# Layer norm, low-rank attention and a mixture of experts on one core: the order of GpSimd's work and of the score pairs, copies two steps later, low-rank rows in one DRAM block, the first steps written out

## The chip, the cores and the metric

One core of a Trainium2 chip runs the whole program. The metric is the device time of one execution in microseconds, the median of several runs. Engines: PE (TensorE), DVE (VectorE), ACT (ScalarE), POOL (GpSimd) and SP (SyncE), which issues most DMAs.

## The reference, cut to what matters

The input x is 8 batches of 512 tokens of width 256. All is float32.

```python
xn = layernorm(x)
def holo_linear(x, basis, phase, amp):           # basis 32x256, phase and amp 256x32
    return (x @ basis.T) @ (amp * cos(phase)).T  # rank 32
q, k, v = (heads(holo_linear(xn, ...)) for each)           # 16 heads of 16
attn = holo_linear(softmax(q @ k.T / 4) @ v, *o)
y = sum over the best 2 of 8 experts: share * (silu(xn @ w_gate) * (xn @ w_up)) @ w_down   # F = 352
shared = (silu(xn @ sw_gate) * (xn @ sw_up)) @ sw_down     # F = 704, every token
out = x + attn + y + shared
```

## The kernel before, in words

The kernel has three stages. **Preparation**: normalised rows go to DRAM (xn_rows) and, transposed and split, to xn_T_split; the tokens are routed and sorted by expert; the last batch's low-rank rows (low_rank_first) and its q and k rows are made. The low-rank rows are the 3 x 32 = 96 products of xn with the bases of q, k and v. Numbers are kept as a high and a low part, and a product takes the pairs high-high, low-high, high-low. **Tiles**: 71 tiles of 128 sorted tokens run through their expert, and expert_rows holds the results. **Attention**: 8 batches (b; the data come last batch first) of 4 head groups (g) of 8 steps (t), called a slot (b, g). `slots` calls one function per engine for (-1, 3), a slot without attention of its own that makes what (0, 0) needs, and then for all others.

In each step PE makes two pairs of score matmuls. The *score pair* (`score`, L1363, into s_pair) holds q times k for a later slot, four steps to a slot ahead; DVE takes its maximum over keys (`maximum`, L1867), and only then may the next score pair start, as there is one s_pair. The *transposed pair* (`score_T`, L1437, into st_pair) holds k times q of the present slot with the maxima as additional rows; ACT takes its exponential (`exponent`, L1082), and only then may the next one start. In before, `next_score` goes first in steps with t % 4 other than 0, and `score_T` first in steps 0 and 4. The matmuls of values with the exponentials (`values`, L1449) are in steps 0 and 4. Between them PE does pieces of the shared SwiGLU of the same or next batch: `gate_up_shared` (L1409) for hidden tiles 0 to 4 of 128 columns, 24 matmuls in 4 pieces over 4 steps, `gate_up_both` for the last tile of 64 ("odd"), then `down_pair` (L1512). Step 2 or 6 also has one small matmul group: a projection of the next batch's q or k (`project`, L1353), the output projection, the low-rank rows of batch b + 2 (`low_rank`, L1463) or the values.

Of a SwiGLU tile q: ACT takes the tanh and a halved copy of `up`, DVE multiplies (`gate_shared`, L1882), POOL multiplies by `up` (`hidden`, L777), ACT copies the high part (`hidden_high`, L1063, in steps 1 and 5), POOL makes the low part (`hidden_low`, L785). Tile 4 of a batch is in slot (b, 1), second half, and so is the odd tile.

POOL's work is one list written by hand: per batch the four `hidden` and `hidden_low`, the gathers of expert rows (`gather_y`, L802, each a DMA that POOL issues), their sums (`sum_y`, L809 to L814), and for each half of the heads `normalise` (L793, after a broadcast of the inverse sums, o_sum, comes back from DRAM) and `ao_low` (L797). Each waits in order.

SP's work is a list too. In slot (b, 3) it stores the high low-rank rows of b + 2 (L607), waits for DVE's low part, stores that (L609), loads the maxima into q_rows (`load_max`, L632, after ACT's copy of the turned maxima at L1041), loads q and k rows three slots ahead (`load_rows`, L557), and reloads the low-rank rows in the layout of the projections (`load_low_rank`, L616), for which it first waits until both stores have landed (semaphore r_st). In `slot_first` it loads rows of group 1, stores low rank 1, loads the maxima, reloads low rank 1 and loads rows of group 2. In the preparation (L504, L507) it does the same two stores, and ACT waits for them before it writes over their source (L940).

Memory: w_sh, xT_b1 and what follows them in the stage `late` lie over the first experts' weights, which are free when the last experts run.

Of the kernel before, what the change touches and what calls it, by code (L numbers as in the profile page):

```python
# [6 lines left out]
P = 128  # L7
# [8 lines left out]
HI, LO = 0, 1  # L16
# [47 lines left out]
def build_program(nc, x, attn, gate_w, w_gate, w_up, w_down, sw_gate, sw_up, sw_down, out):  # L64
# [36 lines left out]
    r_dram = nc.dram_tensor("low_rank_rows", (2, 32, 3, L), F32).ap()  # L101
# [11 lines left out]
    with ctx:  # L113
# [108 lines left out]
        xT_1 = sb("xT_b1", [P, 2, KT, L], F32R, late)  # L222
        r_hi = sb("r_hi", [96, L], F32R, late)
# [6 lines left out]
        q_rows = [None] + [sb(f"q_rows{g}", [P, 2, L], F32R, late) for g in range(1, NG)]  # L230
        k_rows = [None] + [sb(f"k_rows{g}", [P, 2, L], F32R, late) for g in range(1, NG)]
# [176 lines left out]
        def slots(slot):  # L408

            slot(-1, 3)  # L410
            for b in range(NB):
                for g in range(NG):
                    slot(b, g)
# [48 lines left out]
        def _(sp):  # L462
# [44 lines left out]
            sp.dma_start(r_dram[LO].rearrange("h n l -> n h l"), e_lo[0][0:96, :].bitcast(F32)).then_inc(r_st, 16)  # L507
# [52 lines left out]
            def load_first_values():  # L560
                for c, part in enumerate((HI, HI, LO)):
                    sp.dma_start(r_rows[0][c * HARM:(c + 1) * HARM, 2, :].bitcast(F32), r_dram[part, :, 2, :]).then_inc(r_in, 16)
# [41 lines left out]
            def store_low_rank(b):  # L604
                wait(sp, r_in, b * 48)
                wait(sp, a_r, b + 1)
                sp.dma_start(r_dram[HI].rearrange("h n l -> n h l"), r_hi[:, :].bitcast(F32)).then_inc(r_st, 16)  # L607
                wait(sp, d_r, b + 1)
                sp.dma_start(r_dram[LO].rearrange("h n l -> n h l"), r_lo[:, :].bitcast(F32)).then_inc(r_st, 16)  # L609

            def load_low_rank(b):
# [3 lines left out]
                for c, part in enumerate((HI, HI, LO)):  # L615
                    sp.dma_start(r_rows[b % 2][c * HARM:(c + 1) * HARM, :, :].bitcast(F32), r_dram[part]).then_inc(r_in, 16)  # L616
# [99 lines left out]
        def _(pool):  # L716
# [103 lines left out]
            def last_group(b):  # L820
# [7 lines left out]
                if there(b + 1):  # L828
                    hidden_low(b + 1, 0)
                    gather_at(b + 1, 1, 3, 6) if there(b) else gather_y(0, 1)  # L830

            last_group(-1)
            for b in range(NB):
                hidden(b, 1)
                gather_at(b, 2, 0, 1)
                hidden_low(b, 1)
                sum_y(b, 0)
                gather_at(b, 3, 0, 3)
                hidden(b, 2)
                gather_at(b, 4, 0, 5)  # L840
                hidden_low(b, 2)
                sum_y(b, 1)
# [3 lines left out]
                hidden_low(b, 3)  # L846
# [1170 lines left out]
```

## Time and profile before

| | us |
|---|---|
| runs, median (lowest to highest) | 995.96 (995.03 to 998.99) |
| the profiled execution's own time | 991.98 |
| its span, first to last instruction | 990.2 |
| mean granted clock of TensorE, share of 2.4 GHz | 0.950 |
| preparation, up to the first tile | 94 |
| tiles | 278 |
| attention, from its first shared matmul at 374.4 | 616 |

A span is from the first instruction to the last of one profiled execution; the time of that execution has some 2 us around it. An engine's busy time says how much it had to do, and the waits say what it stood for. A busy matmul row is not a matmul at its peak, since ends of pipelined matmuls are modelled.

### The profile page before, as it was taken

Reading aid. Unit: us, or ns where it says so; the run is one execution under the profiler, and the core shown is the slowest. Engines: PE = TensorE matmul, PEld = TensorE weight load, DVE = VectorE, ACT = ScalarE, POOL = GpSimd, SP = SyncE. Lnnn points to the kernel's source line nnn. Section 1 sums busy time; section 2 is a strip of 40 time slices with the busy share of each in tenths; the row PEclk is TensorE's granted clock in tenths of the full one; section 3 lists DMA queues with packets and bytes.
Section 4 is the critical chain, followed back from the end, with each engine's and each line's share of the span. In section 5 each row is a group of like instructions: output and inputs, shape, how many; then the busy total and the mean of one; then the engine's idle time right before and its main releaser. Section 6 shows DMA issues by size and latency. Waiting matters only on the chain.

```text
span 990.2 us, 19557 instructions
## 1 busy us (share of the span) xinstructions
PE 882.8 (89%) x6491; PEld 616.1 (62%) x6492; DVE 613.8 (62%) x923; ACT 580.6 (59%) x935; POOL 407.1 (41%) x411
## 2 busy tenths in 40 slices
PE   4745999999999986999999998989989999989996
PEld 3435999999999974555464464555455555446452
DVE  7867834434443454776776775766766686776762
ACT  4746644444444433757757756756756766766764
POOL 2003522222222233825825815733833752752831
PEclk9965999999999998999999999989999999999999
DMA  9983655222222126464565655554655664644411
GB/s 314 382 253 136 209 144 168 74 73 70 69 74 70 47 91 148 143 166 129 171 173 134 185 153 131 163 154 121 182 153 128 175 167 117 184 125 99 107 31 43
DMA packets 89928, 140.04 MB, mean 141 GB/s; under 512 B 17304, under 2 KB 51616, under 8 KB 87936
## 3 DMA queue, kind: packets, MB, share of 16 engines
q1 hardware_dynamic: 83168, 121.24, 42.4%
q0 software_dynamic: 6480, 17.70, 6.7%
q8 instruction: 44, 0.72, 0.3%
q14 instruction: 28, 0.23, 0.1%
q10 hardware_dynamic: 208, 0.14, 0.0%
HBM read 79.24 MB, written 54.71 MB: 135 GB/s over the span
## 4 chain that ended last, share of the span: by engine, by line
PE 59%; DMA 18%; DVE 7%; POOL 5%; ACT 4%; issue 4%; SPq 3%; DVEq 0%; ACTq 0%; POOLq 0%
PE s_pair L1290 8%; PE bank L1308 8%; PE bank L1512 7%; PE bank L1449 6%; PE st_pair L1290 6%; PE s_pair L1363 4%; PE bank L1409 4%; DMA low_rank_rows<-ro 4%; PE st_pair L1437 4%; DMA r_rows<-low_rank_rows 3%; DMA o_sum<-inverse_rows 3%; DMA inverse_rows<-o_inv 2%; PE bank L1298 2%; DVE top L1867 2%; PE bank L1273 2%
## 5 line engine op out<-in xcount | busy, mean ns | idle before, releaser
L1867 DVE TENSOR_REDUCE top<-s_pair 128x2 f32<-128x1024 f32 x248 | 303.8, 1225 | 166.6 <-PE s_pair L1363 159.0
L1082 ACT ACTIVATE prob<-st_pair 128x1024 f32<-128x1024 f32 x252 | 258.3, 1025 | 109.4 <-PE st_pair L1437 105.6
L755 POOL DMA_INDIRECT xg<-xn_rows,token_of x71 | 78.5, 1106 | 216.7 <-PE bank L1273 161.9
L1409 PE MATMUL bank<-xT_b,w_sh 64*128 64x512 f32 x960 | 146.5, 411 | 0.4
L1363 PE MATMUL s_pair<-k_rows,q_rows 48*128 48x512 f32 x496 | 117.8, 469 | 13.1 <-DVE top L1867 10.8
L1437 PE MATMUL st_pair<-q_rows,k_rows 50*128 50x512 f32 x504 | 109.2, 428 | 19.7 <-ACT prob L1082 11.0
L1449 PE MATMUL bank<-prob,v_ones 128*32 128x512 f32 x1024 | 126.5, 613 | 0.0
L1409 PEld LDWEIGHTS bank<-xT_b,w_sh 64*128 64x128 f32 x960 | 93.6, 191 | 30.7 <-issue 8.4
L793 POOL TENSOR_TENSOR ao<-ao,o_sum 128x512 f32<-128x512 f32 x15 | 19.3, 1287 | 183.6 <-DMA o_sum<-inverse_rows 183.6
L1308 PE MATMUL bank<-w_exp,c_hT 128*128 (+1 forms) x639 | 94.2, 292 | 0.3 <-ACT c_y L994 0.3
L777 POOL TENSOR_TENSOR h_f<-h_f,u_half 128x512 f32<-128x512 f32 x40 | 51.6, 1291 | 92.3 <-DVE h_f L1882 92.0
L1290 PE MATMUL s_pair<-w_exp,xg_T 128*128 x468 | 88.6, 339 | 0.0
L1363 PEld LDWEIGHTS s_pair<-k_rows,q_rows 48*128 48x128 f32 x496 | 48.8, 191 | 63.8 <-DVE top L1867 48.2
L1308 PEld LDWEIGHTS bank<-w_exp,c_hT 128*128 128x128 f32 (+1 forms) x639 | 81.2, 190 | 0.7 <-issue 0.6
L1512 PE MATMUL bank<-w_sh,h_T 64*128 64x256 f32 x1088 | 80.4, 282 | 1.3 <-DVE ro L1934 1.1
L1512 PEld LDWEIGHTS bank<-w_sh,h_T 64*128 64x128 f32 x1088 | 75.0, 185 | 9.9 <-issue 3.0
L1290 PEld LDWEIGHTS s_pair<-w_exp,xg_T 128*128 128x128 f32 x468 | 77.7, 195 | 0.3
L1437 PEld LDWEIGHTS st_pair<-q_rows,k_rows 50*128 50x128 f32 x504 | 49.5, 191 | 42.2 <-ACT prob L1082 20.2
L1290 PE MATMUL st_pair<-w_exp,xg_T 128*128 x384 | 70.7, 333 | 0.0
L989 ACT ACTIVATE c_hT<-bank 128x384 fp32r<-128x384 f32 x71 | 34.9, 491 | 59.3 <-PE bank L1298 59.3
L802 POOL DMA_INDIRECT y_b<-expert_rows,slot_of x64 | 64.1, 1002 | 12.0 <-issue 7.5
L1449 PEld LDWEIGHTS bank<-prob,v_ones 128*32 128x32 f32 x1024 | 27.2, 111 | 62.5 <-issue 57.1
(230 smaller groups left out, 1249.9 us busy)
## 6 DMA issues: line engine op xcount, KB each, us to landing
qk_rows<-qk_hi SPq DMA_DIRECT2D x56, 256.0 KB
q_rows<-qk_rows SPq DMA_DIRECT2D x64, 192.0 KB
k_rows<-qk_rows SPq DMA_DIRECT2D x56, 192.0 KB
expert_rows<-c_y SPq DMA_DIRECT2D x71, 128.0 KB, 1.7
xn_T_split<-x_T SPq DMA_DIRECT2D x8, 1024.0 KB, 6.6
xT_b<-xn_T_split SPq DMA_DIRECT2D x7, 1024.0 KB, 8.6
qk_rows<-qk_lo SPq DMA_DIRECT2D x28, 256.0 KB
x_all<-in_L_attn_x_dram SPq DMA_DIRECT2D x8, 512.0 KB, 8.1
```

The source lines that it names most:

```text
L755: pool.indirect_dma_start(xg[s % 4][:, :], None, xn_dram, bass.IndirectOffsetOnAxis(token_of[:, s:s + 1], 0)).then_inc(c_x[s % 4], 16)
L777: pool.tensor_tensor(h, h, u_half[:, :], ALU.mult).then_inc(p_hf, 1)
L802: pool.indirect_dma_start(y_b[:, t % 2, k, :], None, y_dram, bass.IndirectOffsetOnAxis(slot_of[:, k, of(b) * TPB + t:of(b) * TPB + t + 1], ...
L1082: act.activation(prob[n % 3][:, 2 * jp:2 * jp + 2, :].rearrange("p j l -> p (j l)"), score_T_pair(b, g, t)[:, :], ACT.Exp, scale=HD ** -0. ...
L1290: ins = pe.matmul(gu_bank_of(s, i)[n][:, 0:F], xg_T[i % 2][:, a * KT + k, :], w, start=(m == 0 and k == 0), stop=(m == 2 and k == KT - 1))
L1308: ins = pe.matmul(y_bank[:, 0:D], c_hT[i % 2][0:n, a, k, :], w, start=(m == 0 and k == 0), stop=(m == 2 and k == FT - 1))
L1363: ins = pe.matmul(score_pair(b, g, v)[:, i * 512:(i + 1) * 512], q_rows[g][r:r + 48, jp, qt * P:(qt + 1) * P], k_rows[g][r:r + 48, jp, :], ...
L1409: ins = pe.matmul((g_bank, u_bank)[up][:, :], w_sh[rows, a, o:o + P], xT_of(b)[rows, c, k, :], start=(n == 0 and i == 0), stop=(n == 1 and ...
L1437: ins = pe.matmul(score_T_pair(b, g, t)[:, i * 512:(i + 1) * 512], k_rows[g][r:r + QK_ROWS, jp, kt * P:(kt + 1) * P], q_rows[g][r:r + QK_R ...
L1449: ins = pe.matmul(ot_bank[32 * j:32 * j + 32, :], v_ones[:, kt, 4 * g + j, :], prob[(b * 16 + g * 4 + kt) % 3][:, j, :], start=(kt == 0), ...
L1512: ins = pe.matmul((g_bank, u_bank)[to][:, 0:D], h_T[rows, a, f, t * P:(t + 1) * P], w_sh[rows, c, S_GU + f * D:S_GU + (f + 1) * D], start= ...
L1867: dve.tensor_reduce(top[g % 2][:, :, jp, qt], score_pair(b, g, v)[:, :].rearrange("p (i k) -> p i k", i=2), AX_X, ALU.max).then_inc(d_max, 1)
```

## The change

- r_dram, low_rank_rows, is (2, 96, 512) in place of (2, 32, 3, 512): the stores write it as it lies, and the reload picks rows n * 32 + h.
- q_rows1 and k_rows1 get a place directly behind xT_b1, and load_rows(0, 1) is issued after the store of tile 66, behind load_xT(1).
- POOL: in each batch sum_y(0), sum_y(1) come before hidden_low 1, 2; normalise(b-1, 1) and gather 7 before hidden_low 3; sum_y(2) behind hidden 4 and ao_low; gather 1 of the next batch before its hidden_low 0.
- ACT: hidden_high in steps 3 and 7 in place of 1 and 5.
- PE: score_T first in every step.
- slot(-1, 3) goes; its work is written out for PE, DVE and ACT, and low_rank(1) comes behind turn_max(0, 0) and score(0, 1, 0).

```diff
-    r_dram = nc.dram_tensor("low_rank_rows", (2, 32, 3, L), F32).ap()
+    r_dram = nc.dram_tensor("low_rank_rows", (2, 96, L), F32).ap()
...
         xT_1 = sb("xT_b1", [P, 2, KT, L], F32R, late)
+        q_rows1 = sb("q_rows1", [P, 2, L], F32R, late)
+        k_rows1 = sb("k_rows1", [P, 2, L], F32R, late)
...
         def slots(slot):
 
-            slot(-1, 3)
             for b in range(NB):
...
-            sp.dma_start(r_dram[HI].rearrange("h n l -> n h l"), e_hi[0][0:96, :].bitcast(F32)).then_inc(r_st, 16)
+            sp.dma_start(r_dram[HI], e_hi[0][0:96, :].bitcast(F32)).then_inc(r_st, 16)
...
                 if s == 66:
                     load_xT(1)
+                    load_rows(0, 1)
...
-                sp.dma_start(r_dram[LO].rearrange("h n l -> n h l"), r_lo[:, :].bitcast(F32)).then_inc(r_st, 16)
+                sp.dma_start(r_dram[LO], r_lo[:, :].bitcast(F32)).then_inc(r_st, 16)
...
-                    sp.dma_start(r_rows[b % 2][c * HARM:(c + 1) * HARM, :, :].bitcast(F32), r_dram[part]).then_inc(r_in, 16)
+                    sp.dma_start(r_rows[b % 2][c * HARM:(c + 1) * HARM, :, :].bitcast(F32), r_dram[part].rearrange("(n h) l -> h n l", n=3)).then_inc(r_in, 16)
...
             def slot_first():
-                load_rows(0, 1)
+                load_max(0, 0)
                 store_low_rank(1)
-                load_max(0, 0)
+                load_rows(0, 2)
                 load_low_rank(1)
-                load_rows(0, 2)
...
                 if there(b + 1):
+                    gather_at(b + 1, 1, 3, 6) if there(b) else gather_y(0, 1)
                     hidden_low(b + 1, 0)
-                    gather_at(b + 1, 1, 3, 6) if there(b) else gather_y(0, 1)
...
                 gather_at(b, 2, 0, 1)
+                sum_y(b, 0)
                 hidden_low(b, 1)
-                sum_y(b, 0)
...
                 gather_at(b, 4, 0, 5)
+                sum_y(b, 1)
                 hidden_low(b, 2)
-                sum_y(b, 1)
...
                 gather_at(b, 6, 1, 1)
-                hidden_low(b, 3)
                 if there(b - 1):
                     normalise(b - 1, 1)
-                sum_y(b, 2)
                 gather_at(b, 7, 1, 3)
+                hidden_low(b, 3)
                 hidden(b, 4)
                 if there(b - 1):
                     ao_low(b - 1, 1)
+                sum_y(b, 2)
                 hidden_low(b, 4)
...
-                    if t % 4 == 1 and what == "pair":
+                    if t % 4 == 3 and what == "pair":
                         hidden_high(c, q)
...
+            max_rows(0, 0)
             low_rank_high(1)
-            max_rows(0, 0)
+            tanh(0, 0)
+            up_half(0, 0)
+            values_out(0, 0)
+            hidden_high(0, 0)
             slots(slot)
...
                     score(0, 0, run)
-                    low_rank(1)
                     down(NS - 1, END - 1, at[run + 1])
-                    turn_max(0, 0)
...
                     wait(pe, a_mt, b * NG + 1)
+                    if b == 0:
+                        pe.wait_ge(d_r, 2)
...
                 for t in range(STEPS):
-                    if t % 4:
-                        next_score(b, g, t)
                     if now:
                         score_T(b, g, t)
+                    next_score(b, g, t)
                     if t % 4 == 0:
-                        next_score(b, g, t)
                         piece(b, g, t, 4)
...
             some_tiles(NS // RUN * RUN, last=True)
+            turn_max(0, 0)
+            score(0, 1, 0)
+            low_rank(1)
             pe.wait_ge(c_yk, NS)
             pe.wait_ge(c_hed, NS)
+            for n in range(3):
+                gate_up_shared(0, 0, n)
+            score(0, 1, 1)
+            gate_up_shared(0, 0, 3)
+            score(0, 1, 2)
+            project_values(0, 0)
+            score(0, 1, 3)
+            for n in range(4):
+                gate_up_shared(0, 1, n)
 
             slots(slot)
...
             split_max(0, 0)
+            maximum(0, 1, 0)
             low_rank_low(1)
+            maximum(0, 1, 1)
             dve.wait_ge(c_yk, NS)
             dve.memset(v_ones[:, :, :, HD:2 * HD], 1.0).then_inc(ones_ok, 1)
+            maximum(0, 1, 2)
+            gate_shared(0, 0)
+            maximum(0, 1, 3)
```

## Rows read from the trace of the kernel before

**Rows 1.** The page, part 1: busy us, share of the span, instructions by engine
```profile
PE 882.8 (89%) x6491; PEld 616.1 (62%) x6492; DVE 613.8 (62%) x923; ACT 580.6 (59%) x935; POOL 407.1 (41%) x411
```

**Rows 2.** Windows: stretch, its length, busy us and count by engine, PEclk, DMA share, GB/s
```profile
461.79:914.35 452.56, 419.99 (x3294) 238.52 (x3295) 316.74 (x371) 297.04 (x400) 233.35 (x228) 0.97 0.57 152
914.35:948.77 34.42, 32.03 (x218) 16.06 (x218) 24.13 (x27) 25.47 (x35) 30.32 (x31) 1.00 0.37 93
498.40:516.47 18.07, 17.70 (x202) 12.69 (x203) 14.13 (x19) 10.05 (x12) 2.11 (x3) 1.00 0.62 177
516.47:533.87 17.40, 17.39 (x131) 9.66 (x127) 12.29 (x15) 12.16 (x16) 6.51 (x6) 1.00 0.27 76
```

**Rows 3.** Waits of PE in 388 to 990: us in total, times, longest
```profile
PE st_pair L1437 <- ACT prob L1082: 11.0, 9, 2.2
...
PE bank L1353 <- DMA r_rows<-low_rank_rows: 9.3, 6, 2.3
PE st_pair L1437 <- DMA q_rows<-top_T: 8.3, 6, 2.0
```

**Rows 4.** Timeline of SP: start, us, DMA; the seam from batch 2 to 3
```profile
601.06 0.69 SPq L609 DMA_DIRECT2D low_rank_rows<-ro  x1
603.24 1.48 SPq L632 DMA_DIRECT2D q_rows<-top_T  x2
...
609.09 1.25 SPq L616 DMA_DIRECT2D r_rows<-low_rank_rows  x3
```

**Rows 5.** The page, part 6: DMA issues, KB each, us to landing
```profile
expert_rows<-c_y SPq DMA_DIRECT2D x71, 128.0 KB, 1.7
```

**Rows 6.** Window while the two low-rank stores run, columns as in rows 2
```profile
600.00:606.00 6.00, 6.00 (x47) 2.99 (x45) 4.71 (x8) 4.87 (x9) 2.98 (x3) 1.00 0.22 57
```

**Rows 7.** Timeline of PE at the same seam: start, us, group, idle before and its releaser
```profile
609.76 0.49 PE L1437 MATMUL st_pair<-q_rows,k_rows 50*128 50x512 f32 x2 [1.39 <-DMA q_rows<-top_T]
...
617.33 0.50 PE L1353 MATMUL bank<-r_rows,w_rows 96*128 96x512 f32 x1 [2.27 <-DMA r_rows<-low_rank_rows]
```

**Rows 8.** Timeline of all engines in the preparation
```profile
59.10 0.76 PE L1231 MATMUL bank<-e_qk,w_rows 96*128 96x512 f32 x1 [4.40 <-issue]
...
62.90 1.08 ACT L940 ACTIVATE e_hi<-bank 128x512 fp32r<-128x512 f32 x2 [4.82 <-DMA low_rank_rows<-e_lo]
```

**Rows 9.** Timeline of all engines in slot (3, 1)
```profile
638.77 1.29 POOL L793 TENSOR_TENSOR ao<-ao,o_sum 128x512 f32<-128x512 f32 x1 [2.47 <-DMA o_sum<-inverse_rows]
640.03 1.83 POOL L809 TENSOR_SCALAR y_b<-y_b,share 128x256 f32<-128x256 f32 x2
...
644.69 1.28 POOL L777 TENSOR_TENSOR h_f<-h_f,u_half 128x512 f32<-128x512 f32 x1
...
646.00 0.63 ACT L1063 ACTIVATE h_T<-h_f 128x512 fp32r<-128x512 f32 x1 [3.37 <-POOL h_f L777]
```

**Rows 10.** The page, part 5: DVE's maxima; busy us, mean ns | idle before
```profile
L1867 DVE TENSOR_REDUCE top<-s_pair 128x2 f32<-128x1024 f32 x248 | 303.8, 1225 | 166.6 <-PE s_pair L1363 159.0
```

**Rows 11.** Timeline of PE, steps 3 to 6 of slot (1, 3)
```profile
523.81 0.39 PE L1363 MATMUL s_pair<-k_rows,q_rows 48*128 48x512 f32 x2
...
525.57 0.50 PE L1437 MATMUL st_pair<-q_rows,k_rows 50*128 50x512 f32 x2
525.90 0.40 PE L1363 MATMUL s_pair<-k_rows,q_rows 48*128 48x512 f32 x2
...
528.30 0.50 PE L1363 MATMUL s_pair<-k_rows,q_rows 48*128 48x512 f32 x2
...
530.13 0.50 PE L1363 MATMUL s_pair<-k_rows,q_rows 48*128 48x512 f32 x2
```

**Rows 12.** Timeline of PE, from the last tile to slot (0, 0)
```profile
374.39 3.39 PE L1409 MATMUL bank<-xT_b,w_sh 64*128 64x512 f32 x24
380.02 0.80 PE L1363 MATMUL s_pair<-k_rows,q_rows 48*128 48x512 f32 x2 [2.24 <-DMA q_rows<-qk_rows]
...
388.71 0.40 PE L1437 MATMUL st_pair<-q_rows,k_rows 50*128 50x512 f32 x2
```

More of the change, by code:

```diff
@@ L229, in build_program @@
         qk_lo = [sb(f"qk_lo{i}", [P, L], F32R, late) for i in range(2)]
-        q_rows = [None] + [sb(f"q_rows{g}", [P, 2, L], F32R, late) for g in range(1, NG)]
-        k_rows = [None] + [sb(f"k_rows{g}", [P, 2, L], F32R, late) for g in range(1, NG)]
+        q_rows = [None, q_rows1] + [sb(f"q_rows{g}", [P, 2, L], F32R, late) for g in range(2, NG)]
+        k_rows = [None, k_rows1] + [sb(f"k_rows{g}", [P, 2, L], F32R, late) for g in range(2, NG)]
         u_half = sb("u_half", [P, L], F32, late)
@@ L561, in load_first_values @@
                 for c, part in enumerate((HI, HI, LO)):
-                    sp.dma_start(r_rows[0][c * HARM:(c + 1) * HARM, 2, :].bitcast(F32), r_dram[part, :, 2, :]).then_inc(r_in, 16)
+                    sp.dma_start(r_rows[0][c * HARM:(c + 1) * HARM, 2, :].bitcast(F32), r_dram[part, 2 * HARM:3 * HARM, :]).then_inc(r_in, 16)
             def store_y(s, i):
@@ L1114, in slot @@
                         up_half(c, q)
-                    if t == 5 and there(nb) and now:
+                    if t == 5 and there(nb):
                         max_rows(nb, ng)
@@ L1133, in slot @@
                         qk_high(b + 1, PROJECTED.index((g, t)))
-                    if g == 3 and t == 2 and there(b + 2) and now:
+                    if g == 3 and t == 2 and there(b + 2):
                         low_rank_high(b + 2)
@@ L1369, in turn_max @@
                 more = there(b + 1)
-                if g == 0:
+                if (b, g) == (0, 0):
+                    pe.wait_ge(c_hed, NS - 1)
+                elif g == 0:
                     wait(pe, d_r, b + 2) if more else wait(pe, d_po, (b - 1) * 2)
@@ L1456, in low_rank @@
                 wait(pe, xT_in, b * 16)
-                if b == 2:
-                    wait(pe, a_mt, 4)
+                if b <= 2:
+                    wait(pe, a_mt, 1 if b == 1 else 4)
                 else:
@@ L1568, in next_score @@
                 if t < STEPS - AHEAD:
-                    if there(nb) and there(b):
+                    if there(nb):
                         score(nb, ng, t + AHEAD)
@@ L1593, in small @@
                     project_o(b - 1, t // 4)
-                if g == 3 and t == 2 and there(b + 2) and there(b):
+                if g == 3 and t == 2 and there(b + 2):
                     low_rank(b + 2)
@@ L1614, in slot @@
                         values(b, g, 1)
-                    if t == 4 and there(nb) and now:
+                    if t == 4 and there(nb):
                         turn_max(nb, ng)
@@ L1939, in slot @@
                     if t < STEPS - AHEAD:
-                        if there(nb) and now:
+                        if there(nb):
                             maximum(nb, ng, t + AHEAD)
@@ L1943, in slot @@
                         maximum(qb, qg, t - STEPS + AHEAD)
-                    if t == STEPS - AHEAD - 1 and there(nb) and now:
+                    if t == STEPS - AHEAD - 1 and there(nb):
                         split_max(nb, ng)
@@ L1959, in slot @@
                         qk_low(b + 1, PROJECTED.index((g, t - 1)))
-                    if g == 3 and t == 3 and there(b + 2) and now:
+                    if g == 3 and t == 3 and there(b + 2):
                         low_rank_low(b + 2)
```

4 lines of the change are left out of this document (2 added, 2 removed).

## The prediction

> **What bounds the kernel now.** I read the page first, then the PE's waits in the attention phase, then windows of one batch, then the timelines round each wait. PE is busy 89% of the span; no other engine is over 62% [rows 1]. So time can only be had where PE stands still or has to go slower, and the windows say how much that is. Batches 1 to 6 take 452.56 us, 75.4 each. The same 32 steps without a stop are found in pieces: groups 0 and 1 in batch 7 (34.42), group 2 of batch 1 (18.07), group 3 of batch 1 up to its last wait (17.40), together 69.9 [rows 2]. Six times 75.4 minus 69.9 is **33 us** of stops and of half-speed PE behind them, for these six batches.
>
> The waits name three of the stops [rows 3]: the transposed score pair for ScalarE's exponential (11.0 us, 9 times), the first projection of the next batch for its low-rank rows (9.3, 6 times), the transposed pair for the maxima in q_rows (8.3, 6 times). Once or twice a batch each: these are seams, not the regular step. They sum to 28.6, and a granted clock of 0.97 in the mean, where 1.00 is 2.4 GHz [rows 2], holds most of the remainder of the 33.
>
> **Low-rank rows in one DRAM block.** At the end of a batch SP stores the high half, waits, stores the low half at 601.06, issues the maxima at 603.24 and can issue the reload only at 609.09, since it waits for the stores to land [rows 4]: 8 us for 192 KB. A 128 KB store of expert rows lands in 1.7 us [rows 5]. From 600 to 606 us the DMA share is 0.22, and the stream is little else than these two stores [rows 6]: 3 of 16 engines would be 0.19. The stored view is (3, 32, 512). The changed one is (96, 512). What it will use no row of before shows.
> The Trainium skill, "DMA: Bandwidth & Descriptors", section on why a DMA increments by 16, lets the slowest dimension of both access patterns set the number of engines, the largest divisor up to 16: 3 before, 16 after. The trace agrees with its first half (0.22 against 3/16).
> The bounds of one store are 1.7 us (the expert rows) and the present 8. I take 2.5: same size and shape class as the expert rows, half as large again. The reload then goes out straight behind the row loads, about 607 in place of 609.09, and the three stores' engines are free for the maxima. The reload itself turns from 6 KB into 2 KB pieces with 32 partitions outermost as before; I cost that between -0.5 and +1 us a batch, at 0.
> - Maxima: issued at 603.24, they held the pair until 609.76, after 1.39 idle [rows 7]. Two or three us of landing make them early by 2: all of 8.3 goes. SP's issue time doesn't move, since it waits for ScalarE's copy.
> - Projection: stopped 2.27 until 617.33 [rows 7]. Without the first stop PE is there at 613.7 (617.33 - 2.27 - 1.39); the reload, issued at 607 and landing 8 us later as now, would still be 1.3 late, and with less queued before it about in time. I let 2 of the 9.3 us stand.
> - Once more in the preparation: ScalarE stood 4.82 us for the low store, until 62.90, while the PE's first projection it copies ended at 59.10 + 0.76 [rows 8]. It starts at 59.9: **3.0 us**, and the inversion chain, the gathers and the tiles behind it all start from there. Bounds: 0, if another load is as late; 4.8, if the operands come earlier too.
>
> **GpSimd's order and the copies two steps later.** In group 1, GpSimd's normalise waits 2.47 for o_sum and ends at 640.06; then come the sum of expert rows from 640.03 on, a gather, and the product for SwiGLU tile 4 only at 644.69, so ScalarE, in order, stands 3.37 before its copy at 646.00 with the exponentials of two steps behind it [rows 9]. The new order puts before that product, after the same normalise, only gather 7 and hidden_low 3. The latter is 1.3, a tile like the products; the gather at most 1.5, what the 4.66 from 640.03 to 644.69 leave after 1.83 for two products and two additions of half a tile (0.65 each). So it begins by 642.9 and ends by 644.1. And the copy is asked for after the exponential of step 7, two steps or 4 us later (69.9 / 32 is 2.2 a step). So the stop of 3.37 has 1.8 + 4 to hide in. Late next are: ao_low for the output projection in step 7 (644.1 + 1.3 = 645.4, where it now ends at 647.3), hidden_low 4 behind the sum (3.2 and 1.3 more, 649.9; needed in step 2 of group 2, some 3 us later), and tanh of the odd tile, which needs hidden_low 3 (642.9, asked for in step 6). All pass, the first by the least. GpSimd's total is unchanged. The 11.0 us go, and I keep 1 us for a batch in which o_sum is later.
>
> **The transposed pair first.** Costed at nothing, by the steps themselves. DVE's maximum takes 1.23 us [rows 10], and score pair to score pair takes at least 1.82 (528.30 to 530.13) [rows 11]. Now the pair goes from step 3 to step 4 in 2.09 (523.81 to 525.90), since the transposed pair of step 4 goes ahead; afterwards by 1.82: 0.27 won. At step 4 to 5, 2.40 now, a transposed pair (0.33, 525.57 to 525.90) gets ahead: 0.33 lost [rows 11]. Net +0.06 for a half slot, up to 62 of them: +4. Where step 3 is bound otherwise, the 0.27 may be more or less. I take 0, bounds -5 and +20 (the 0.33 lost 62 times, nothing won).
>
> **First steps written out.** From the first shared gate matmuls to the first transposed pair PE takes 14.3 us (374.39 to 388.71) [rows 12]. Of that 6.8 are the two tiles' 48 matmuls (3.39 each) and about 1.6 four score pairs and the values; 5.9 are waits, 2.24 of them for q_rows that SP loads only after the last expert rows, and half-speed matmuls (a pair at 0.80 [rows 12], elsewhere 0.50 [rows 11]). The loads move ahead into tile 66; four DMAs of 0.4 us (three take 1.25 [rows 4]) between two stores cost nothing, since a tile takes 278 / 71 = 3.9. Low rank 1 moves from before the last down projection to behind the maxima's turn: neutral, and its cover is DVE's reading of the next scores. New waits: four maxima (4 x 1.23), a memset, the low-rank difference and one gate run in one DVE chain, with PE between them; I count 1 to 1.5 us of PE idle. Gain **5**, bounds 1 and 7.
> Of the queues: SP now issues the maxima of group 0 first, then the two low-rank stores, the rows of group 2, and the reload; the row loads (four, 0.4 each) cover the stores' landing, on which SP stood before. The values' projection gets a wait for DVE's low-rank difference, since both use one bank; it stands two score pairs behind it in the order, so it is costed at nothing, and 1 us if DVE is late.
>
> **The sum**, against the profiled execution's own 991.98 (span 990.2): preparation -3, first steps -5, seam waits 8.3 + 7.3 + 10 = -25.6, half-speed stretches that followed them -3 (of the 33 - 28.6 = 4.4), order 0. **-37, that is 955.** The runs' median, 995.96, is 4 above the profiled one; half of that may be its own. I say **958**.
>
> **Rivals.**
> - *Half the seams stay* (0.22). The reload still comes late, or o_sum does, which GpSimd waits for in every batch. For: both are behind the loads of q and k rows, and a faster PE asks sooner. Against: the copies have 4 us to spare. 25.6 / 2 or 13 us come back, and 1 for the clock: 972.
> - *The first steps run at half speed* (0.06). Their gaps are about 1.5 us in 12; the same work before, with 2.24 in one piece, had pairs of 0.80. Then 6.8 us of gate matmuls take some 4 more, and the gain is 1: 962. The Trainium skill, "TensorE: Matmul & The Clock Gate", Part 1, calls the slow clock the default, which activity releases; it would expect this wherever PE has been idle for long. The trace agrees here with its slow pairs behind the 2.24 us.
> - *The store stays on few engines* (0.05). 8.3 + 9.3 + 3 and some clock stay: 980. Against: the view's outer dimension is plainly 96.
> - *Every wait goes, with the half-speed stretches behind them* (0.15). All 33, and 6 to 7 before: 946.
> - *No net gain* (0.04). Maxima and waits eat it: 990 to 995.
> - *Slower: DVE's chain takes over* (0.04). With pairs evenly spaced, DVE's other work (the gate at steps 0 and 4, differences at 3 and 7) falls between maxima. Place: the score pair of those 4 steps of 8 in 32 slots. Against: steps 0 and 4 have 2.4 us of other matmuls. It decides from 37 / 128 = 0.29 us for each; at 0.45 it adds 58, so 1013 with 955 for the rest.
>
> **Numbers.** The main case has 0.44. Measurement tells 0.5% (5 us) from no change. Faster 0.92 (main case and the first four rivals), same 0.04, slower 0.04. Range 944 to 976: from the case with all waits gone to the one with half the seams, with 2 and 4 us beyond them for the medians; the stores' case and the last two, 0.13, lie outside.
>
> **What would show it.** The reload's issue 2 us nearer to the maxima's, DMA share over 0.5 just after each store; no wait on low-rank stores in the preparation, ScalarE's first copy at 60. PE's waits on the maxima gone, on low-rank rows under 3, on the exponential under 2. First transposed pair at about 381 (388.7 - 3 - 5). Score pair to score pair from step 3 to 4 at 1.82. Batches near 71. Wrong: a batch still over 74, or new waits on GpSimd's low halves in the down projection, or on the score pair in every step.

## The result, and the profile after

The changed kernel takes **957.61 us** (median of 4 runs, 956.90 to 959.46), the kernel before 995.50 (4 runs, 993.93 to 998.99): ratio 0.9618, 95% interval 0.9589 to 0.9647. The profiled execution took 956.90, its span is 955.0. The forecast was 958.

The page's first part, to lay beside [rows 1]:

```profile
PE 876.5 (92%) x6491; PEld 613.0 (64%) x6492; DVE 617.5 (65%) x923; ACT 580.7 (61%) x935; POOL 405.9 (43%) x411
```

The same work in a shorter span. The window of batches 1 to 6, then the two stores of low-rank rows (columns as in [rows 2] and [rows 6]):

```profile
454.98:879.42 424.44, 412.62 (x3296) 236.39 (x3296) 318.10 (x372) 297.14 (x402) 235.01 (x228) 1.00 0.62 162
...
589.40:590.70 1.30, 1.28 (x13) 0.74 (x10) 1.23 (x3) 0.94 (x2) 0.00 (x0) 1.00 0.52 151
591.80:593.20 1.40, 1.40 (x15) 0.34 (x9) 1.38 (x2) 1.10 (x3) 0.00 (x0) 1.00 0.48 135
```

A batch takes 70.7 us in place of 75.4 (69.72, 73.76, 70.49, 70.34, 70.09, 70.05: the second is the odd one), and the granted clock is 1.00 in place of 0.97. PE's waits, 388 to 955 us, beside [rows 3]:

```profile
PE st_pair L1442 <- ACT prob L1083: 5.8, 10, 1.1
PE bank L1356 <- DMA r_rows<-low_rank_rows: 4.6, 4, 3.1
PE bank L1519 <- DVE ro L1951: 2.9, 7, 0.5
```

The wait on the maxima (q_rows) is gone, the one on low-rank rows is halved, and most of what is left of it (3.1 of 4.6) is one stop in batch 2. Two things have to be added. The window of [rows 3] begins just before the first transposed pair of before (388.71); in the changed kernel that pair comes at 382.61, so a window from 388 us leaves out one more stop for the exponential, and from the first transposed pair on that wait is 8.8 us, not 5.8:

```profile
386.30 0.50 PE L1442 MATMUL st_pair<-q_rows,k_rows 50*128 50x512 f32 x2 [3.05 <-ACT prob L1083]
```

And before had a wait of the same size as the three of [rows 3], which they leave out. It is PE's for DVE's maxima; 0.7 us of it are left:

```profile
PE s_pair L1363 <- DVE top L1867: 9.5, 16, 1.3
```

SP at the seam from batch 2 to 3, beside [rows 4], and the landing of the stores in the view of DMA issues:

```profile
591.48 0.31 SPq L611 DMA_DIRECT2D low_rank_rows<-ro  x1
593.48 1.32 SPq L634 DMA_DIRECT2D q_rows<-top_T  x2
...
596.78 1.31 SPq L618 DMA_DIRECT2D r_rows<-low_rank_rows  x3
```

```profile
low_rank_rows<-r_hi SPq DMA_DIRECT2D x7, 192.0 KB, 2.1
```

The DMA share during the two stores is 0.52 and 0.48, before 0.22 [rows 6]. The reload goes out 5.3 us after the low store, before 8.0 [rows 4]. In the preparation ScalarE no longer stands for a store, beside [rows 8]:

```profile
58.60 0.60 ACT L941 ACTIVATE e_hi<-bank 128x512 fp32r<-128x512 f32 x1 [0.76 <-PE bank L1236]
59.37 0.60 ACT L941 ACTIVATE e_hi<-bank 128x512 fp32r<-128x512 f32 x1 [0.17 <-PE bank L1236]
```

### The profile page after: what moved, and what is told of

The parts are those of the page before. It is cut to its first block, busy times and chain, and to the rows that moved or that the text cites. A ratio compares the mean times of both kernels' runs of the same rounds, so it can differ in the third digit from the quotient of the medians.

```text
span 955.0 us, 19558 instructions
## 1 busy us (share of the span) xinstructions
PE 876.5 (92%) x6491; PEld 613.0 (64%) x6492; DVE 617.5 (65%) x923; ACT 580.7 (61%) x935; POOL 405.9 (43%) x411
## 4 chain that ended last, share of the span: by engine, by line
PE 72%; DVE 13%; DMA 6%; issue 3%; ACT 3%; SPq 2%; POOL 0%; DVEq 0%; ACTq 0%
PE bank L1414 10%; PE bank L1454 9%; PE bank L1313 8%; PE s_pair L1295 8%; PE bank L1519 7%; PE s_pair L1366 6%; PE st_pair L1442 6%; PE st_pair L1295 6%; DVE top L1884 4%; DMA r_rows<-low_rank_rows 4%; PE bank L1303 2%; PE bank L1278 2%; PE bank L1427 1%; ACT prob L1083 1%; PE bank L1468 1%
## 5 line engine op out<-in xcount | busy, mean ns | idle before, releaser
L756 POOL DMA_INDIRECT xg<-xn_rows,token_of x71 | 76.1, 1072 | 217.4 <-PE bank L1278 165.3
L1454 PE MATMUL bank<-prob,v_ones 128*32 128x512 f32 x1024 | 123.5, 600 | 0.0
L1442 PE MATMUL st_pair<-q_rows,k_rows 50*128 50x512 f32 x504 | 112.2, 440 | 8.9 <-ACT prob L1083 8.8
L1366 PE MATMUL s_pair<-k_rows,q_rows 48*128 48x512 f32 x496 | 113.3, 451 | 2.6 <-DVE top L1884 1.8
L1856 DVE TENSOR_TENSOR xg_T<-bank,xg_T 128x256 fp32r<-128x256 f32 x71 | 30.1, 424 | 56.2 <-ACT xg_T L980 53.0
```

The costliest lines, as they stand in the source:

```text
L756: pool.indirect_dma_start(xg[s % 4][:, :], None, xn_dram, bass.IndirectOffsetOnAxis(token_of[:, s:s + 1], 0)).then_inc(c_x[s % 4], 16)
L1366: ins = pe.matmul(score_pair(b, g, v)[:, i * 512:(i + 1) * 512], q_rows[g][r:r + 48, jp, qt * P:(qt + 1) * P], k_rows[g][r:r + 48, jp, :], ...
L1442: ins = pe.matmul(score_T_pair(b, g, t)[:, i * 512:(i + 1) * 512], k_rows[g][r:r + QK_ROWS, jp, kt * P:(kt + 1) * P], q_rows[g][r:r + QK_R ...
L1454: ins = pe.matmul(ot_bank[32 * j:32 * j + 32, :], v_ones[:, kt, 4 * g + j, :], prob[(b * 16 + g * 4 + kt) % 3][:, j, :], start=(kt == 0), ...
```

## The experiments

All keep the computation. They ran on three chips, each beside the kernel before: the block's three and "row load late" on one, the next four rows of the table on a second, "first steps undone" and the last three on a third. The changed kernel ran with the result alone. The kernel before had medians of 995.5 us with the result and 997.5, 1001.4 and 999.0 on the three chips, so a difference of up to some 6 us between a kernel's median and the changed kernel's 957.61 is not told from none by medians alone. The ratios, each to before on the same chip, are a second measure, and the stages of the profiled executions, one for each kernel, a third. The last three columns split the profiled execution: where the first gather starts (the preparation), from the end of DVE's last instruction on a tile to the first transposed pair (the first steps), and from there to the end (attention). The tiles between the first two took 278.6 to 280.7 us in all of them.

| kernel | us, median (range) | ratio to before, 95% | first gather | first steps | attention |
|---|---|---|---|---|---|
| before | 995.50 (993.9 to 999.0) | | 89.0 | 19.9 | 601.5 |
| changed | 957.61 (956.9 to 959.5) | 0.962 (0.959 to 0.965) | 86.1 | 15.8 | 572.4 |
| before, block alone | 976.20 (973.8 to 978.4) | 0.980 (0.975 to 0.986) | 86.2 | 20.1 | 586.1 |
| block undone | 980.77 (977.4 to 983.1) | 0.983 (0.977 to 0.989) | 90.4 | 15.9 | 594.9 |
| block of 6 x 16 (two runs) | 968.89 (964.8 to 973.0) | 0.972 (0.964 to 0.981) | 86.6 | 15.8 | 581.2 |
| GpSimd's order undone | 979.38 (977.5 to 983.2) | 0.980 (0.974 to 0.985) | 85.4 | 16.0 | 595.8 |
| late copies undone | 974.90 (968.6 to 980.2) | 0.972 (0.966 to 0.978) | 85.4 | 15.8 | 597.1 |
| both undone | 974.77 (972.1 to 977.0) | 0.975 (0.970 to 0.981) | 85.6 | 16.0 | 590.1 |
| pair order undone | 955.36 (952.2 to 958.5) | 0.954 (0.950 to 0.958) | 85.7 | 16.0 | 575.6 |
| first steps undone | 959.89 (959.0 to 964.9) | 0.962 (0.958 to 0.967) | 86.3 | 20.3 | 572.5 |
| row load late | 964.95 (964.1 to 966.0) | 0.969 (0.963 to 0.974) | 86.1 | 23.8 | 573.2 |
| reload first | 950.57 (946.6 to 951.6) | 0.951 (0.948 to 0.954) | 86.3 | 16.1 | 568.3 |
| reduction for copy | 954.49 (952.8 to 956.5) | 0.956 (0.952 to 0.959) | 85.0 | 14.6 | 575.6 |
| both of these | 952.83 (949.7 to 953.9) | 0.954 (0.951 to 0.957) | 86.4 | 15.8 | 566.7 |

### The DRAM block: alone, undone, and with six pieces

```diff
 # alone, in the kernel before (undone: the reverse, in the changed kernel)
-    r_dram = nc.dram_tensor("low_rank_rows", (2, 32, 3, L), F32).ap()
+    r_dram = nc.dram_tensor("low_rank_rows", (2, 96, L), F32).ap()
```

> The kernel before with the (2, 96, 512) block alone. Theory (the stores ran on few engines, and the seam waits on the maxima and the low-rank rows come from that): those two waits fall from 8.3 and 9.3 to 0 and about 3, the preparation gets 3 shorter, ScalarE's wait for GpSimd's hidden tile (17.5 us, 8 times) stays: 996 - 8.3 - 6 - 3 = 978, and as much off for the half-speed stretches behind the stops, 976 to 980. Rival (the stops are one slack: with the copies still held up, the time comes back at the next one): 985 to 992, with PE's wait for the exponential up from 11 to 20 us.

> The changed kernel with the (2, 32, 3, 512) block back. Theory: the two stores land late again, PE waits again 8 us on the maxima and 9 on low-rank rows, the preparation is 3 longer: 957.6 + 20 = 976 to 980. Rival (in the changed order of work the pair goes first, and the seam has room for the landing): under 966, the preparation's 3 and the low-rank rows' 5 alone.

Alone it gives 21.3 us on one chip (976.20 against 997.48), and taking it out of the changed kernel costs 23.2. The two agree, and both lie where the theory put them (980.77 is 0.8 over its upper bound). PE's waits with the block undone:

```profile
PE bank L1356 <- DMA r_rows<-low_rank_rows: 11.5, 6, 2.7
PE st_pair L1442 <- DMA q_rows<-top_T: 8.8, 6, 2.0
```

Both are back, the preparation is 4.3 longer, and the granted clock falls to 1.2 GHz behind the stop in each of batches 2 to 6 (in the changed kernel in batch 2 alone). The rival is out: no slack elsewhere takes the stops up, though ScalarE's wait on `hidden` did grow in the kernel with the block alone (20.1 us, 16 times; before 17.5, 8 times).

```diff
-    r_dram = nc.dram_tensor("low_rank_rows", (2, 96, L), F32).ap()
+    r_dram = nc.dram_tensor("low_rank_rows", (2, 16, 6, L), F32).ap()
 # stores: r_dram[part].rearrange("h n l -> n h l"); the reload in six DMAs of 16 partitions
```

> The changed kernel with the block as (2, 16, 6, 512), stored as (6, 16, 512): the outermost dimension is 6, and a reload takes six DMAs of 16 partitions in place of three of 32. Theory (the outermost dimension sets the number of engines, and the time follows it): while a store runs the DMA share is 6/16 = 0.37, and its landing takes half of what the (3, 32, 512) view took; the maxima are early enough, the low-rank rows some 2 us a batch late, 965 to 970. Rival (any view that jumps in DRAM is slow, whatever its outermost dimension): as slow as the kernel with the block undone, 976 to 980, share 0.2. Third (the outermost dimension doesn't matter as long as the pieces are spread): no difference from the changed kernel but the three more issues, 957 to 960.

The low half is stored at 593.15, and its semaphore's last event in the trace is at 597.11, 4.0 us later. With (3, 32, 512) that took 7.8 (599.70 to 607.48, block undone), with (96, 512) 2.1. The low store waits behind the high one, which SP issued 2.5 us earlier; the high store alone took 6.5 with 3, 4.0 with 6 and 2.1 with 96 (6.4 to 6.8, 4.0 to 4.4 and 2.1 over the six seams from 440 us on). So the time of the same 192 KB falls as the outermost dimension goes 3, 6, 96: the first theory. The rival (any view that jumps is slow) is out, and so is the third. The trace shows the number of engines too, in the events of the stores' semaphore: 4, 7 and 16 for one store, that is one soon after the issue and 3 or 6 landings, or 16 landings. The Trainium skill, "DMA: Bandwidth & Descriptors", section "Why a DMA increments its semaphore by 16 and not by 1", gives 3, 6 and 16 engines for these, the largest divisor up to 16, and the counts of landings agree with it. The time falls less than the count grows: by the count alone 6.5 would become 3.3 and 1.2, where 4.0 and 2.1 were measured, so a part of the time does not shrink with it. The DMA share was less than expected, 0.22 and 0.32 in the two stores. The maxima's wait is 0.7, once. But this kernel isn't a clean price of the stores: SP needs longer for six issues, and PE waits 10.8 us for low-rank rows although the stores landed in time:

```profile
597.48 0.90 SPq L558 DMA_DIRECT2D q_rows<-qk_rows  x2
598.50 3.77 SPq L622 DMA_DIRECT2D r_rows<-low_rank_rows  x6
```

```profile
607.32 0.50 PE L1360 MATMUL bank<-r_rows,w_rows 96*128 96x512 f32 x1 [1.79 <-DMA r_rows<-low_rank_rows]
```

### GpSimd's order and the later copies, one by one

```diff
 # GpSimd's order undone: as before in every batch, e.g.
-                    normalise(b - 1, 1)
-                gather_at(b, 7, 1, 3)
                 hidden_low(b, 3)
+                    normalise(b - 1, 1)
+                sum_y(b, 2)
+                gather_at(b, 7, 1, 3)
 # late copies undone
-                    if t % 4 == 3 and what == "pair":
+                    if t % 4 == 1 and what == "pair":
```

> The changed kernel with GpSimd's old order, the copies still in steps 3 and 7. Theory (the stop of 3.37 before the copy has 4 us to hide in by the two later steps alone): within 2 us of 957.6, and what is late is the odd tile's tanh or ao_low. Rival (both are needed: sums and the low half ahead of hidden 4 hold it up by 3.8 us and with what follows the copy, hidden_low 4 comes too late for the down projection): 963 to 970, a wait of PE on hidden_low of 1 us and more for each batch.

> The changed kernel with the copies of the high part in steps 1 and 5 again, GpSimd in its new order. Theory (the new order brings hidden 4 from 644.7 to 642.9, so 1.8 of the 3.37 us go and 1.6 stay before the copy, with the exponentials behind it): ScalarE's wait on hidden back at 6 to 10 us over 8 batches, 961 to 965. Rival (what stops ScalarE is gone with GpSimd's order): 956 to 959.

> The changed kernel with both GpSimd's old order and the copies in steps 1 and 5. Theory (the 11.0 us of PE's wait for the exponential come back): 957.6 + 10 = 966 to 969, ScalarE's wait on hidden at 15 to 20 us. Rival (with the pair first there is more room before the transposed pair, or the stops fall together with those at DVE): 958 to 962.

**Each half alone is worth nothing.** Without both 974.8, with the new order alone 974.9, with the late copies alone 979.4, with both 957.6. That last kernel ran on another chip than the three, but "pair order undone", which has both halves and ran beside the three, took 955.36. My theories for the single halves fell, and that for both undone (966 to 969) was 6 us short. Three mechanisms show.

The new order alone moves the stop from one tile to another. In slot (3, 1) of that kernel, GpSimd, ScalarE and PE:

```profile
626.81 1.28 POOL L778 TENSOR_TENSOR h_f<-h_f,u_half 128x512 f32<-128x512 f32 x1
```

```profile
628.12 0.63 ACT L1064 ACTIVATE h_T<-h_f 128x512 fp32r<-128x512 f32 x1 [2.14 <-POOL h_f L778]
628.66 0.58 ACT L1069 ACTIVATE v_ones<-bank 128x512 f32<-128x512 f32 x1
```

```profile
629.29 0.79 PE L1356 MATMUL bank<-r_rows,w_rows 96*128 96x512 f32 x1 [2.08 <-ACT v_ones L1069]
```

Now it is tile 3 whose product is late, since 3.4 us of sums stand before `hidden_low` 2 and it, and GpSimd had first stood 1.99 us for the gathered rows that they read. ScalarE stands, its copy of the values with it, and PE stands for that bank: a wait of 9.8 us in all that the kernel before had once, with 0.9.

The late copies alone turn the wait round. GpSimd makes the low half of what ScalarE copies, so it waits for the copy, 54.1 us in 31 waits (7.8 in 11 in the changed kernel), and what is behind it on GpSimd is late. PE's waits (the turning of the maxima for a bank that DVE reads, and the output projection for ao_low):

```profile
PE bank L1383 <- DVE qk_lo L1877: 6.0, 6, 1.7
PE bank L1553 <- POOL ao_T L798: 5.8, 7, 2.8
```

The output projection is what the prediction named as next to be late. The wait for DVE is something else: released by ScalarE's copy in step 3, GpSimd now runs tile after tile just when DVE splits the maxima. The timeline of all engines in slot (4, 0), DVE's and GpSimd's rows:

```profile
702.37 2.86 DVE L1891 CAST top_parts<-top 128x16 fp32r<-128x16 f32 x1
...
702.62 1.29 POOL L786 TENSOR_TENSOR h_T<-h_f,h_T 128x512 fp32r<-128x512 f32 x1
...
703.86 1.27 POOL L794 TENSOR_TENSOR ao<-ao,o_sum 128x512 f32<-128x512 f32 x1
...
705.11 1.83 POOL L810 TENSOR_SCALAR y_b<-y_b,share 128x256 f32<-128x256 f32 x2
```

A copy of 128 x 16 numbers, 0.17 us otherwise, takes 2.86. DVE's two instructions of the split take 34.4 us in this kernel, 21.8 in the changed one, 16.7 before.

### The order of the pairs

```diff
                 for t in range(STEPS):
+                    if t % 4:
+                        next_score(b, g, t)
                     if now:
                         score_T(b, g, t)
-                    next_score(b, g, t)
                     if t % 4 == 0:
+                        next_score(b, g, t)
```

> The changed kernel with the old order of the pairs: the score pair first in steps with t % 4 other than 0. Theory (costed at nothing, 0.27 won and 0.33 lost for a half slot): 957.6 within 3 us either way; score pair to score pair goes from 1.74 to about 2.0 between steps 3 and 4, and from 2.6 to 2.4 between steps 4 and 5. Rival (the transposed pair first lets ScalarE's exponential start a pair earlier, and this is what took its stops away): PE's wait for the exponential up from 8.8 to 15 or more, 965 to 972. Second rival (the new order costs DVE's chain time): 947 to 953.

955.36 against 957.61, on different chips, with ranges that overlap; by the ratios the old order is 0.8% the faster (0.950 to 0.958 against 0.959 to 0.965), by the attention stage of the two profiled executions the new one by 3.2 us. The measures differ in sign, so what the order is worth is not shown, and the old one may be the better. The two orders trade one wait for another, from 388 us on: PE stands 9.1 us for DVE's maxima and 1.3 for the exponential with the old order, 0.7 and 5.8 with the new. The changed kernel's score pairs in slot (1, 3), steps 3 to 5, beside [rows 11]:

```profile
515.00 0.40 PE L1366 MATMUL s_pair<-k_rows,q_rows 48*128 48x512 f32 x2
...
516.81 0.50 PE L1366 MATMUL s_pair<-k_rows,q_rows 48*128 48x512 f32 x2
...
519.65 0.39 PE L1366 MATMUL s_pair<-k_rows,q_rows 48*128 48x512 f32 x2
```

1.81 and 2.84, where 1.82 and 2.73 (2.40 and 0.33) were forecast from 2.09 and 2.40.

### The first steps

```diff
 # first steps undone: slot(-1, 3) back on PE, DVE and ACT, load_rows(0, 1) back in slot_first
+            slot(-1, 3)
             for b in range(NB):
 # row load late: only the load
                 if s == 66:
                     load_xT(1)
-                    load_rows(0, 1)
...
             def slot_first():
+                load_rows(0, 1)
                 load_max(0, 0)
```

> The changed kernel with slot (-1, 3) back in all engines, the rows of group 1 loaded in slot_first and low rank 1 before the last down projection. Theory (the first steps gave 3.2 us, the remainder of what the first transposed pair came earlier after the preparation's 2.9): 960 to 962, first transposed pair at about 386. Rival (part of the 3.2 is only moved, since slot (0, 0) is no shorter than before and waits 3 us for its fifth exponential): 957 to 959.

> The changed kernel with the rows of group 1 loaded in slot_first, behind the last store of expert rows, in place of behind tile 66's store. Theory (that load was the one long stop of the first steps, 2.24 us, with slow matmuls behind it): the first transposed pair comes 2 to 4 us later than 382.6, 960 to 961.5. Rival (the maxima chain of the written-out steps is what bounds them, so the load is hidden): 957 to 958.5, first transposed pair within 1 us.

Undone, the first steps take 20.3 us in place of 15.8, and nothing changes behind them (572.5 against 572.4): 4.5 us, not given back in these two executions. Nine kernels with the written-out steps and the early load take 15.8 to 16.1 us for them (a tenth 14.6), so the 4.5 is clear of noise in the stage; the medians of two chips differ by 2.3 and the ratios by nothing (0.962 both). The load alone is worth more than the whole: with it late they take 23.8, and the time is 7.3 longer. The theory for it (2 to 4 us, 960 to 961.5) was too small: the first transposed pair comes at 389.05, 6.4 later, and the median is 964.95.

```profile
374.51 0.79 PE L1366 MATMUL s_pair<-k_rows,q_rows 48*128 48x512 f32 x2 [6.46 <-DMA q_rows<-qk_rows]
```

The written-out order asks for these rows straight behind the last tile; the old one did 24 gate matmuls first, so that the same landing cost 2.24 [rows 12]. Written out, but without the early load, they would be 3.5 us slower than the old ones (23.8 against 20.3).

### Two repairs

The stop that is left in batch 2, in SP's timeline of the changed kernel, and with the reload first:

```diff
-                if there(rb):
-                    load_rows(rb, rg)
 # the reload of the low-rank rows stays here, in the third group
+                if there(rb):
+                    load_rows(rb, rg)
```

> The changed kernel with SP's reload of the low-rank rows ahead of the load of q and k rows, in the third group of each batch. Theory (the reload stands behind four issues that take 1.4 to 3.7 us, and PE waits 4.6 us in 4 seams for it): that wait goes to under 1 us, 953 to 956, most of it in batch 2. Rival (the q and k rows, now later by the three reload issues, or by a wait for the stores' landing, are late for a score pair): a new wait on q_rows, 957 to 962.

```profile
521.48 0.80 SPq L558 DMA_DIRECT2D k_rows<-qk_rows  x2
522.33 2.31 SPq L558 DMA_DIRECT2D q_rows<-qk_rows  x2
524.75 1.31 SPq L618 DMA_DIRECT2D r_rows<-low_rank_rows  x3
```

```profile
522.07 1.36 SPq L618 DMA_DIRECT2D r_rows<-low_rank_rows  x3
523.54 1.65 SPq L558 DMA_DIRECT2D k_rows<-qk_rows  x2
525.23 0.91 SPq L558 DMA_DIRECT2D q_rows<-qk_rows  x2
```

PE's wait on low-rank rows is gone, and no wait on q_rows has come: the theory, with more gained than it had (953 to 956). Batch 2 takes 69.65 in place of 73.76, and the span from the first transposed pair on is 4.1 shorter. At 950.57 this is the fastest kernel of the case; its interval (0.948 to 0.954) lies under that of the changed kernel (0.959 to 0.965). The 7.0 us between the two medians are of two chips; on its own chip it is 9.3 under "first steps undone", and with the 4.5 us of those steps taken off, 4.8, which is near the 4.1 of the spans. The q and k rows are needed three slots later, the low-rank rows in two steps.

```diff
-                dve.tensor_copy(dst[:, :, HI, :, :], src).then_inc(d_mh, 1)
+                dve.tensor_reduce(dst[:, :, HI, :, :].rearrange("p i j t -> p i (j t)"),
+                                  src.rearrange("p i j (t r) -> p i (j t) r", r=1), AX_X, ALU.max).then_inc(d_mh, 1)
```

> The changed kernel with DVE's copy in split_max (the high part of the maxima, 128 x 16) written as a maximum over an axis of one element; the values are the same. Theory (DVE's copy and GpSimd's instruction can't run side by side: the copy, 0.17 us alone, took 1.27 to 1.30 in five slots in which the normalise had just begun, and ended with it; a reduction doesn't wait): no such row over 0.4 us, the 14.1 us of these rows down to 6, the fifth to sixth transposed pair in slot (b, 1) 2.25 in place of 2.82, 953 to 956. Rival (the reduction is held as well, or the delay is hidden by PE's other work): 957 to 958.5.

> The changed kernel with the reload first and the copy as a maximum. Theory (the two stops are in different slots, groups 3 and 1): the gains add, 949 to 954. Rival (they share one slack, DVE's chain of maxima): no faster than the better of the two alone.

DVE and GpSimd in slot (3, 1) with the reduction:

```profile
622.79 0.17 DVE L1891 TENSOR_REDUCE top_parts<-top 128x16 fp32r<-128x16 f32 x1
622.99 0.93 DVE L1894 TENSOR_TENSOR top_parts<-top,top_parts 128x16 fp32r<-128x16 f32 x1
```

```profile
622.60 1.29 POOL L794 TENSOR_TENSOR ao<-ao,o_sum 128x512 f32<-128x512 f32 x1 [1.09 <-DMA o_sum<-inverse_rows]
```

The reduction runs in 0.17 in the midst of the normalise, as the theory had it (32 of them take 5.4 us, the copies 14.1). But then the subtraction behind it, which reads two operands from SBUF, is held until the normalise ends: its 32 take 12.6 in place of 7.7. The hold moved one instruction on. The fifth to the sixth transposed pair in slot (3, 1) takes 2.50 in place of 2.86, and attention isn't shorter, 575.6 against 572.4. The median is 3.1 lower, on another chip, and the profile has that ahead of attention (85.0, 14.6), so nothing shows a gain from the edit, though the median lies in the theory's range. Both repairs together are no faster than the reload alone (952.83 and 950.57, same chip, overlapping).

## Why the prediction was right, and where its steps were off

The time came out 0.4 us from the forecast, and the seams it named are where the time was. That it came so close is in part luck: the working of one term did not hold, a wait of 9.5 us was left out, and errors of several us cancel.

- **Low-rank rows in one block** (3 + 8.3 + 7.3 = 18.6, with a part of the clock's 3): right in mechanism and place. A store lands in 2.1 where 2.5 was taken; the maxima's wait is gone; the first gather comes 2.9 earlier where 3.0 was taken; of the wait on low-rank rows 4.6 stay where 2 were left. The two runs price the block at 21.3 and 23.2, somewhat over the term. The half-speed stretches account for part of this where the block is undone (six from 387 us to the end of batch 6, the changed kernel two). The block alone leaves seven of the eight of before, so it removes them only together with the other parts.
- **GpSimd's order and the late copies** (10): worth 17.2, and wrong in its working. The forecast let the stop of 3.37 hide in 1.8 us from the order and 4 from the copies, two gains that add. The runs show none that add: alone the one moves the stop to tile 3, and the other makes GpSimd wait for ScalarE, a wait that the forecast doesn't have. As far as the waits tell, together the sums fill the time in which GpSimd would wait for the late copy, and the copy gives the products the time that the sums take. The term came out because it was taken from PE's wait as a whole and not from its two parts. PE's wait for the exponential from 388 us on is 16.7 us without both and 5.8 with them; of the remainder of the 17.2, 2.9 are the wait on the values' bank, and there is, as the window of batches 1 to 6 has it, a granted clock of 0.98 against 1.00:

```profile
453.24:893.29 440.05, 415.40 (x3297) 238.08 (x3296) 316.09 (x372) 296.84 (x401) 234.38 (x229) 0.98 0.60 156
```

Where 1 us of the wait for the exponential was to stay, 8.8 did, from the first transposed pair on. Of these 3.05 are in slot (0, 0), where the second transposed pair comes 3.7 us after the first in both kernels: that stop the change left as it was.

- **Half-speed stretches** (3): too small, by the counts. From 387 us to the end of batch 6 the changed kernel has two stretches at 1.2 GHz, the kernel before eight, and the parts' prices exceed their waits by some of this; what each stretch cost is not measured.
- **First steps** (5, bounds 1 and 7): 4.1 against the kernel before (19.9 and 15.8), 4.5 by undoing them. The first transposed pair comes at 382.61, for which 381 was forecast. Missing is what the rival had named, in small: DVE's chain stops PE for 1.06, and the 24 matmuls behind it take 4.64 in place of 3.39, most of it at half speed.

```profile
377.55 0.72 PE L1366 MATMUL s_pair<-k_rows,q_rows 48*128 48x512 f32 x2 [1.06 <-DVE top L1884]
378.13 4.64 PE L1414 MATMUL bank<-xT_b,w_sh 64*128 64x512 f32 x24
382.61 0.40 PE L1442 MATMUL st_pair<-q_rows,k_rows 50*128 50x512 f32 x2
```

- **The transposed pair first** (0): right by the gaps of the steps; the run neither confirms nor refutes the 0. Left out was the wait that the order acts on, PE's for DVE's maxima: 9.5 us before, 9.1 with the old order put back, 0.7 with the new, which in turn has more wait for the exponential.
- **The sum**: by medians the parts undone one by one give 23.2 + 17.2 + 2.3 - 2.2 = 40.5, against 37.9 measured and 37 forecast. By the ratios the same four are 21, 13, 1 and -8, together 27. So the block and the copies with GpSimd's order are clear by either measure, the two others are not, and that the parts add up to the whole is not shown. The terms that were too small (block, copies) and too large (first steps, the waits said to go) nearly cancel.
- **The prices of rivals**: 946 for "every wait goes" can't be followed from the rows. Read as the stops of batch 0, before the window of [rows 2], its 6 to 7 us are too much: that batch took 73.1 us (388.71 to 461.79), 3.2 over the 69.9 without a stop.
- **The rivals**: of the 28.6 us of the three waits 13.4 are left (8.8 and 4.6), where 3 were forecast, yet not half of the gain is missing. Most of the 5.8 us for the exponential behind 388 us go with the pair order: with the old one there are 1.3. DVE's chain takes nothing over: the page has 1.8 us of PE's waiting for the maxima, where before had 9.5 in attention. Not every wait went: batch 2 keeps 4.1 us.

## What to carry to other kernels

A DRAM layout is chosen for the outermost dimension of the view that the slow side moves: 3 pieces, 6 pieces and 96 rows of the same 192 KB landed in 6.5, 4.0 and 2.1 us. Where two engines hand a tile back and forth in order, a later copy and other work before the wait belong together; here the other work alone gained nothing, the later copy alone lost 5 us, and both together gained 13 to 17. On a queue, the load that is needed in two steps goes before the one that is needed in three slots: 4 us for a swap of two lines. A table of waits is to be read whole: the wait that was left out here was the second largest.

## What the runs showed of the hardware that was not expected

**A small copy on DVE can stand for as long as a GpSimd instruction runs.** In the changed kernel, slot (4, 1):

```profile
694.20 1.27 DVE L1891 CAST top_parts<-top 128x16 fp32r<-128x16 f32 x1
695.51 0.17 DVE L1893 TENSOR_TENSOR top_parts<-top,top_parts 128x16 fp32r<-128x16 f32 x1
...
697.33 0.68 DVE L1899 SCALAR_TENSOR_TENSOR h_f<-h_f,bank 128x512 f32<-128x512 f32 x1
```

```profile
694.16 1.28 POOL L794 TENSOR_TENSOR ao<-ao,o_sum 128x512 f32<-128x512 f32 x1 [0.42 <-issue]
...
696.60 1.28 POOL L786 TENSOR_TENSOR h_T<-h_f,h_T 128x512 fp32r<-128x512 f32 x1
```

The copy begins 0.04 us after the normalise and ends with it. Of the 32 copies in the changed kernel 14 begin while a GpSimd tensor instruction runs, and all 14 end 0.03 us after that ends; the other 18 take 0.17 or 0.18. It isn't so in every case: in the kernel before 8 of 11 such copies end with GpSimd's instruction, and two of the other three began in the scaling of expert rows (L809). Eight of the 32 take over 0.6 us in the changed kernel, two in the kernel before, and in four of the eight GpSimd's normalise is what runs: its new place put it on the split of the maxima, which the prediction doesn't have. That this cost any time is not shown; the run with the reduction gained none in attention. The subtraction is held too (0.93 with the reduction ahead of it). The reduction is not, and neither is an instruction that reads one operand from SBUF and one from PSUM: the one at 697.33 takes its usual 0.68 while a low half runs. The Trainium skill, "SBUF — State Buffer", section "Who interferes with whom", says this: the pair of ports that both engines share is an exclusive lock; a copy in a mode that uses both ports and a GpSimd instruction shut each other out for the whole of the one that came first, an instruction with two inputs in SBUF contends with GpSimd's reads, and one with at most one input in SBUF (outside those modes) and, on this chip, a reduction do not. The traces agree in each of the four (1.27, 0.93, 0.17, 0.68). The hold of 2.86 us is in the run with GpSimd's order undone alone, which has one more like it (2.97 us at 848.80): the copy begins in the last 0.25 us of a gather on GpSimd (701.61 to 702.60) and stands through the two tensor instructions behind it. In the changed kernel a copy that began in a gather took 0.18, and why these two were held is open.
